# A fused two-layer decoder on one core: wide adds of GpSimd put on VectorE, the smaller expert scaled by the ratio of the weights, an output bias folded into a weight

## The reference

```
x = LN(x + scan_layer(x))          # in-projection, conv of 4 taps, selective scan over 16 states x 512 channels, out-projection
x = LN(x + cosine_scores(x, ctx))  # a 256x256 matrix of normalized dot products
x = LN(x + experts(x))             # softmax over 4 experts, the best 2 kept
x = LN(x + rotary_attention(x))    # 16 query heads, 4 key heads, width 64, low-rank terms
x = LN(x + cross_attention(x, ctx))
x = LN(x + gated_recurrence(x))    # c = f*c + i*g over the 8 batches; h = tanh(x wo' + c_final uo' + bo)
```

```
# experts: w is the softmax probability of the two best experts, 0 elsewhere
h   = relu(x Wi' + (x A_e') B_e')            # per expert e, width 1024
out = sum_e w_e * (h_e Wo')
# rotary: x1, x2 are the even and odd elements of a head
x1*cos - x2*sin , x1*sin + x2*cos
# cross attention: softmax(q k') v Wo + bo
```

## Time and profile before

| what | us |
| --- | --- |
| median of 3 runs | 1455.17 |
| lowest and highest | 1453.09, 1457.04 |
| the profiled execution's own time | 1455.81 |
| its span, first to last instruction | 1454.0 |
| PE busy / DVE busy / ACT busy / POOL busy in the span | 1267.8 / 1085.2 / 750.3 / 278.8 |
| mean granted TensorE clock | 0.945 of full |

### The profile page before, as it was taken

One profiled execution on the slowest core, in us unless ns is written; L12 is line 12 of the kernel. 1 busy time (PEld: TensorE's weight loads), 2 busy tenths in 40 slices (PEclk: granted clock), 3 DMA queues, 4 the chain that ended last, 5 costly groups with the idle time before them and its releaser, 6 DMA issues.

```text
span 1454.0 us, 17342 instructions
## 1 busy us (share of the span) xinstructions
PE 1267.8 (87%) x6336; PEld 1023.8 (70%) x6336; DVE 1085.2 (75%) x1750; ACT 750.3 (52%) x1637; POOL 278.8 (19%) x239
## 2 busy tenths in 40 slices
PE   3687788899999999999999999999998999899852
PEld 2454556677778787878787777878786878678732
DVE  2799699789977887788959988788778794333216
ACT  1543356365556655664647555665566454534421
POOL 0000124113301242112301231124211330130011
PEclk8877799999999999999999999999999999999967
DMA  4620110201020001100030102010010000000301
GB/s 162 218 76 19 48 38 30 65 1 58 1 99 1 30 30 35 65 30 29 8 92 1 59 0 99 1 30 30 27 66 30 30 8 26 1 0 8 114 0 58
DMA packets 27780, 62.63 MB, mean 43 GB/s; under 512 B 2360, under 2 KB 13720, under 8 KB 27056
## 3 DMA queue, kind: packets, MB, share of 16 engines
q1 hardware_dynamic: 27696, 61.53, 12.6%
HBM read 55.48 MB, written 6.04 MB: 42 GB/s over the span
## 4 chain that ended last, share of the span: by engine, by line
PE 46%; DVE 35%; issue 7%; ACT 7%; POOL 4%; DMA 1%; DVEq 0%; SPq 0%; ACTq 0%; POOLq 0%
PE bank L281 12%; DVE scans L491 10%; PE bank L442 7%; DVE scans L487 6%; PE bank L1066 4%; DVE scans L494 4%; PE bank L1111 4%; PE bank L624 3%; PE bank L1084 3%; PE bank L848 3%; DVE conv L381 2%; DVE nmax L1203 2%; PE bank L842 2%; PE bank L1073 2%; PE bank L579 1%
## 5 line engine op out<-in xcount | busy, mean ns | idle before, releaser
L491 DVE TENSOR_TENSOR_SCAN scans<-scans 128x1024 f32<-128x1024 f32 x128 | 303.2, 2368 | 7.2 <-ACT scans L465 4.9
L465 ACT ACTIVATE scans<-dt,a_neg 128x255 f32<-128x255 f32 x512 | 221.8, 502 | 111.6 <-DVE scans L491 111.4
L442 PE MATMUL bank<-scans,ident 128*128 128x256 f32 x1024 | 261.9, 402 | 19.3 <-DVE scans L494 19.2
L442 PEld LDWEIGHTS bank<-scans,ident 128*128 128x128 f32 x1024 | 198.1, 201 | 56.1 <-DVE scans L494 29.4
L487 DVE TENSOR_TENSOR scans<-conv,BC 128x1024 f32<-128x1024 f32 x128 | 168.3, 1315 | 24.6 <-PE bank L442 20.7
L1147 ACT ACTIVATE ya<-bank,nmax 128x256 f32<-128x256 f32 x256 | 107.0, 469 | 135.2 <-DVE nmax L1203 134.3
L494 DVE TENSOR_TENSOR scans<-scans,BC 128x1024 f32<-128x1024 f32 x128 | 168.9, 1319 | 2.1
L1203 DVE TENSOR_REDUCE nmax<-bank 128x2 f32<-128x512 f32 x128 | 87.4, 683 | 88.4 <-PE bank L1066 88.3
L1084 PE MATMUL bank<-v,ya 128*128 128x65 f32 x1024 | 129.1, 270 | 0.0
L1084 PEld LDWEIGHTS bank<-v,ya 128*128 128x128 f32 x1024 | 125.8, 193 | 1.7 <-issue 0.9
L778 POOL TENSOR_TENSOR wa<-wa 128x512 f32<-128x512 f32 x32 | 61.8, 1940 | 241.0 <-ACT wa L676 240.9
(11 more groups left out here) (255 smaller groups left out, 2192.0 us busy)
## 6 DMA issues: line engine op xcount, KB each, us to landing
BC<-xpj_scratch SPq DMA_DIRECT2D x32, 1024.0 KB, 5.4
xin<-in_x SPq DMA_DIRECT2D x8, 256.0 KB, 2.8
conv<-in_x SPq DMA_DIRECT2D x8, 256.0 KB, 2.8
out<-scans SPq DMA_DIRECT2D x8, 256.0 KB, 2.6
kept_x<-x SPq DMA_DIRECT2D x7, 256.0 KB, 2.0
kept_w<-wa SPq DMA_DIRECT2D x7, 256.0 KB, 2.1
BC<-kept_w SPq DMA_DIRECT2D x1, 1792.0 KB, 9.2
scans<-kept_x SPq DMA_DIRECT2D x1, 1792.0 KB, 13.4
```

The costliest lines, as they stand in the source:

```text
L442: last = pe.matmul(sums_of(c), ident[:, :], hb[u % 2][:, i, :], start=False, stop=(h == UH - 1 and i == HN - 1), skip_group_check=True)
L465: ins = act.activation(dA[u % 2][:, j, 1:S], dt[b % 2][:, c, 1:S], ACT.Exp, scale=a_neg[:, c, n:n + 1])
L491: dve.tensor_tensor_scan(flat(H[:, :, :]), flat(dA[u % 2][:, :, :]), flat(H[:, :, :]), 0.0, ALU.mult, ALU.add).then_inc(s["a_scan"], 1)
```

## The change

The experts' sum moves to VectorE. The second expert, whose weight is the smaller, is now made first: ScalarE writes relu of it times the ratio of the second weight to the first (with the largest logit subtracted, the best expert's exponential is 1, so the second largest exponential is that ratio). The best expert comes second, unscaled, and VectorE makes `max(z, 0) + hid` from the bank in one instruction. The best weight is applied at the residual, which becomes two instructions, one for each tile of tokens. ScalarE's second relu and GpSimd's add are gone, and the scores are no longer divided by their sum.

The rotary sums move to VectorE too. The two instructions of the sine half become one with a reversed middle axis, and the table `rope` is wider.

The output bias of the cross attention is added once, at the start, to row 64 of the second half of `w_vo`, which meets a feature that is always 1; the rows of the softmax sum to 1. GpSimd's add of the bias and its wait are gone.

All five strings of `ORDER` are new.

```diff
-                    act.activation(hid[:, j % 2, :], WB[j % 2][:, :], ACT.Relu, scale=sc2[:, 3, t:t + 1]).then_inc(s["f_r1"], 1)
-                    act.activation(r2[:, j % 2, :], WB[j % 2][:, :], ACT.Relu, scale=sc2[:, 5, t:t + 1]).then_inc(s["f_r2"], 1)
+                act.activation(hid[:, j % 2, :], WB[j % 2][:, :], ACT.Relu, scale=sc2[:, 5, j // 2:j // 2 + 1]).then_inc(s["f_r1"], 1)
...
-            own.link(dve.tensor_reduce(sc2[:, 1, :], sm[:, 1, :, :], AX, ALU.add))
-            own.link(dve.reciprocal(sc2[:, 2, :], sc2[:, 1, :]))
-            own.link(dve.tensor_tensor(sm[:, 2, :, :], sm[:, 1, :, :], wide(2), ALU.mult))
+            own.did(dve.tensor_reduce(sc2[:, 1, :], sm[:, 1, :, :], AX, ALU.add))
...
+            for j in range(4):
+                dve.wait_ge(*of("f_z2_ps", b, j + 1))
+                dve.scalar_tensor_tensor(hid[:, j % 2, :], WB[j % 2][:, :], 0.0, hid[:, j % 2, :], ALU.max, ALU.add).then_inc(s["f_h"], 1)
+                yield
...
-            dve.tensor_tensor(flat(x3[b % 2][:, :, :]), w0[:, :], flat(xb[:, :, :]), ALU.add).then_inc(s["f_res"], 1)
+            for t in range(T):
+                last = dve.scalar_tensor_tensor(x3[b % 2][:, t, :], w0[:, t * D:(t + 1) * D], sc2[:, 2, t:t + 1], xb[:, t, :], ALU.mult, ALU.add)
...
-                pool.tensor_tensor(hid[:, j % 2, :], hid[:, j % 2, :], r2[:, j % 2, :], ALU.add).then_inc(s["f_h"], 1)
...
-            pool.tensor_tensor(x4b[:, :, :], x3[b % 2][:, :, :], b_o1[:, :].unsqueeze(1).to_broadcast([P, T, D]), ALU.add).then_inc(s["c_x4b"], 1)
...
-                    pe.wait_ge(*of("t_rot", b, 6 + 3 * (n - 1)))
+                    pe.wait_ge(*of("t_rot", b, 4 + 2 * (n - 1)))
...
-                dve.tensor_tensor(out_sin[:, :, 0, :], x[:, :, 1, :], neg.to_broadcast(per), ALU.mult).then_inc(s["t_rot"], 1)
-                dve.tensor_tensor(out_sin[:, :, 1, :], x[:, :, 0, :], sin.to_broadcast(per), ALU.mult).then_inc(s["t_rot"], 1)
+                turned = x.rearrange("p h (b r) -> p h b r", b=2)[:, :, ::-1, :]
+                dve.tensor_tensor(out_sin.rearrange("p h (b r) -> p h b r", b=2), turned, sin.rearrange("p h (b r) -> p h b r", b=2),
+                                  ALU.mult).then_inc(s["t_rot"], 1)
...
+                    dve.tensor_tensor(keys[:, :, 0:S], cos_k, sin_k, ALU.add).then_inc(s["t_kr"], 1)
+                    dve.tensor_tensor(keys[:, :, S:S + HD], cos_k[:, :, 0:HD], sin_k[:, :, 0:HD], ALU.add).then_inc(s["t_kr"], 1)
...
+                    dve.tensor_tensor(queries[n % 2], rot[n % 2][:, 0, :], rot[n % 2][:, 1, :], ALU.add).then_inc(s["t_ro"], 1)
...
+            own.link(dve.tensor_copy(flat(w_vo[:, :, :]), w1[:, :]))
+            of_ones = w_vo[CTX - P:CTX - P + 1, 1, :]
+            dve.tensor_tensor(of_ones, of_ones, b_o1, ALU.add).then_inc(s["prep_evac"], 1)
...
     "pool": (
-        "FFFSWWWWWWFWYYYYYSWWWWWWWWYWWYYYYWYFSWWWWWWWWYWWYYYYYWFSWWWWWWWWYWWYYYYWYSFWWWWWWWWYWWYYYYWYFSWWWWWWWWYWWYYYYY"
-        "WSWWWWWWWWYWWYYYYYWSWWWWWWWWYWWYYYYYWWYWWWWW"
+        "FFFSWWWFSWWYFWWWWSWWYWWWFWSWWWWYWWFSWWWWYWWFSWWYWWWWSWWWWYWWSWWWWYWWWYWWWW"
```

More of the change, by code:

```diff
@@ L213, in build @@
         lowT = sb("lowT", [P, 2, S], F32R)
-        x4b, vo, qk, pe_c, pT_c, x1n = [wa[:, 2 * i:2 * i + 2, :] for i in range(6)]
+        vo, qk, pe_c, pT_c, x1n = [wa[:, 2 * i:2 * i + 2, :] for i in range(1, 6)]
+        b_o1 = wa[CTX - P:CTX - P + 1, 8, :]
         tg = wa[:, 0:6, :].rearrange("p (g k) s -> p g k s", g=3)
@@ L682, in kept_hidden @@
                                ACT.Copy).then_inc(s["f_hT"], 1)
-            weighed(0, 0)
+            second_expert(0)
             yield
-            weighed(1, 0)
+            second_expert(1)
             yield
-            for j in range(4):
-                weighed(j, 1)
+            for j in range(1, 4):
+                kept_hidden(j - 1)
                 yield
-                if j >= 1:
-                    kept_hidden(j - 1)
+                if j < 3:
+                    second_expert(j + 1)
                     yield
-                    if j < 3:
-                        weighed(j + 1, 0)
-                        yield
             kept_hidden(3)
@@ L735, in x_dve @@
             dve.wait_ge(*of("f_exp", b))
-            own.link(dve.tensor_reduce(sc2[:, 1, :], sm[:, 1, :, :], AX, ALU.add))
-            own.link(dve.reciprocal(sc2[:, 2, :], sc2[:, 1, :]))
-            own.link(dve.tensor_tensor(sm[:, 2, :, :], sm[:, 1, :, :], wide(2), ALU.mult))
-            for i, (score, hit, rank, one) in enumerate([(2, 3, 4, 5), (6, 7, 8, 9)]):
+            own.did(dve.tensor_reduce(sc2[:, 1, :], sm[:, 1, :, :], AX, ALU.add))
+            for i, (score, hit, rank, one) in enumerate([(1, 3, 4, 5), (6, 7, 8, 9)]):
                 top, best = 3 + 2 * i, 4 + 2 * i
@@ L746, in x_dve @@
                 if i == 0:
-                    own.link(dve.scalar_tensor_tensor(sm[:, 6, :, :], sm[:, 5, :, :], -2.0, sm[:, 2, :, :], ALU.mult, ALU.add))
+                    own.link(dve.scalar_tensor_tensor(sm[:, 6, :, :], sm[:, 5, :, :], -2.0, sm[:, 1, :, :], ALU.mult, ALU.add))
+                    own.did(dve.reciprocal(sc2[:, 2, :], sc2[:, 1, :]))
                 yield
-            own.link(dve.tensor_tensor(sm[:, 10, :, :], sm[:, 9, :, :], sm[:, 5, :, :], ALU.subtract))
+            own.link(dve.tensor_tensor(sm[:, 10, :, :], sm[:, 5, :, :], sm[:, 9, :, :], ALU.subtract))
             for t in range(T):
-                for i, one in enumerate([5, 10]):
+                for i, one in enumerate([9, 10]):
                     own.did(dve.tensor_tensor(low[:, i, t, :].rearrange("p (e r) -> p e r", e=NE),
@@ L762, in x_dve @@
                 dve.wait_ge(*of("l_kept_x", b - 2))
-            dve.tensor_tensor(flat(x3[b % 2][:, :, :]), w0[:, :], flat(xb[:, :, :]), ALU.add).then_inc(s["f_res"], 1)
+            for t in range(T):
+                last = dve.scalar_tensor_tensor(x3[b % 2][:, t, :], w0[:, t * D:(t + 1) * D], sc2[:, 2, t:t + 1], xb[:, t, :], ALU.mult, ALU.add)
+                if t == T - 1:
+                    last.then_inc(s["f_res"], 1)
+                else:
+                    own.did(last)
+            own.wait()
             dve.wait_ge(*of("f_res", b))
@@ L774, in x_pool @@
             yield
-            for j in range(4):
-                pool.wait_ge(*of("f_r1", b, j + 1))
-                pool.wait_ge(*of("f_r2", b, j + 1))
-                pool.tensor_tensor(hid[:, j % 2, :], hid[:, j % 2, :], r2[:, j % 2, :], ALU.add).then_inc(s["f_h"], 1)
-                yield
             pool.wait_ge(*of("x_var", b, 2))
```

126 lines of the change are left out of this document (54 added, 72 removed).

## The result

| | before | changed |
| --- | --- | --- |
| median, us (9 runs each) | 1454.59 | 1450.63 |
| lowest and highest | 1452.48, 1459.87 | 1449.38, 1451.40 |
| span of the profiled execution | 1454.0 | 1448.7 |

The ratio is 0.9968, with an interval of 0.9955 to 0.9980. The change brings 4.0 us by the medians, 4.7 by the ratio, 5.3 by the two spans, where 10.2 was forecast. The sign and the range hold the result; the size does not fit. What follows shows that this is the difference of two larger numbers: the edits alone are worth 14.4 us (13.8 by the ratio), and the new order takes some 10 of them away (9.7 by the medians, 9.2 by the ratios, with some 3 us either way).

A forecast was written before the change was run, and what follows sets the result against it. VectorE was taken to bound the kernel up to 275 us, TensorE after. VectorE's work +5.8, GpSimd's wait -12, ScalarE -3.0, experts' choice -1 make -10.2 on 1455.8: forecast 1445 us, 8-in-10 range 1427 to 1467.

The forecast's parts named there:

- VectorE's prices: Sums and products moved to VectorE: 0.69 us per 512-wide sum, reversed product at the straight price, 46.2 us added in all.
- Lengthening: Scan, L494 and L487 on VectorE: GpSimd's wide adds stretch them by 34.6 us, all given back; VectorE's net +11.6 us.
- rival A: GpSimd's small instructions keep part of the lengthening, only 15.3 of 34.6 us come back: 1455 us, chance 0.22.
- half of VectorE's time: VectorE has 35% of the chain and is 75% busy, so half of net +11.6 us sets the end: +5.8 us.
- GpSimd's wait, -12: TensorE's idle time ended by GpSimd's wide adds, 17.8 us: two thirds should go, -12 us, bounds 0 and -17.8.
- The sum without the order: Whole kernel: +5.8 - 12 - 3.0 - 1 = -10.2 us, with the new order costed at nothing.
- ScalarE and the choice: 32 relus gone from ScalarE, -3.0 us; two small dependent instructions gone ahead of the experts' low-rank product, -1 us.
- The order at nothing: New order strings of all engines: claimed to say the same where they count, 0 us, with 10 us to either side.
- The sign I had set for it: TensorE's start-up stretch ending later than 275 us by more than VectorE's added work there would show the order's doing.
- Rival B: Experts' sums wait for TensorE at the head of VectorE's list, some 0.69 us each: slower, 1472 us, chance 0.20.
- Rival C: All 17.8 us of waits go and scans on the path regain the whole 34.6: 1423 us, chance 0.08.

The follow-up runs named there:

- the idle adds: All edits in the old order, plus GpSimd wide multiplications nobody waits for at its adds' former places: 1470.11 us, against 1440.98 without them.
- all six kernels of the table: Before, changed, three steps put back, old start with new rest, new start with old rest, all old: 89.2 to 90.1 us for this stretch.

## Why the prediction was half right

**VectorE's prices: right.** The sums were put at 0.69 and measure 0.692 and 0.678; the reversed product was taken at the straight price and measures 0.680 against 0.681. VectorE's busy time was to be near 1097 and is 1087.8, 9 us less. Counted over all its kinds, each instruction that GpSimd ran beside less the median of those it did not, the lengthening before was 37.8 us rather than the 34.6 of the three kinds. The other 6 us of the difference were not followed.

**Lengthening: the mechanism right, its share of the path probably too small.** All of it went, as forecast, and rival A's shared lengthening does not exist: the small instructions on GpSimd stretch nothing. But half of VectorE's time was taken as on the path for both signs. For the added sums that nearly holds, 0.39 to 0.45 of 37.7 us. For the stretching by the idle adds it does not: 31.9 us cost 27.6, a share of 0.87. I read this as a matter of place, without a run of its own: the idle adds run where the experts and the rotary part go on, and the instruction they stretch there is one that TensorE's L442 waits for or that the next step of these parts stands behind. The 9.5 us in the sums of the keys are a case of it. In the kernel before, these sums were on GpSimd and 35.6 of the 37.8 us lay in the scan's three kinds, so 0.87 is not measured for its lengthening.

**GpSimd's wait, -12: its sum with the lengthening right, its own size not shown.** Taking the adds away brings 29.5 us where lengthening and wait were to make 29.3. That the sum fits says nothing on its terms. If the lengthening before cost 0.87 of itself, as the idle adds' does, it cost more than 29.5 alone and the waits were worth about nothing; the fit would be luck. If it cost the 0.45 of plain work, 17 us, the waits were worth the 12 of the forecast. No run separates the two. The two engines holding each other is also in the waits: the experts' add took 1.94 us on average, from 1.27 to 3.15, because it was held. The bias add L982, of the same size, always took 1.27 us; VectorE ran beside six of its eight, but only the products L1170, L1172 and L1173, which read one input from PSUM.

**The sum without the order: 10.2 forecast, 14.4 measured.** With the measured pieces it closes better: -29.5 for the adds, 0.39 to 0.45 of 46.2 (+18.0 to +20.8) for the work that VectorE gets, -3.0 and -1 as forecast for ScalarE and the choice: -15.5 to -12.7. The last two were not tried by themselves. The edits brought 4.2 us more than forecast; of that the added work accounts for 2.3 to 5.1, since 18.0 to 20.8 us stand where half of 46.2, 23.1, was put.

**The order at nothing: wrong, and this is the step that failed.** "The order strings are new, but where they count they say the same. ... I cost the new order at nothing, with 10 us to either side." The comparison was made by the place of three things among VectorE's scans: two residuals, of batch 0 and of batch 6, and the last scan. None of them looks at what TensorE does ahead of the first scan, nor at the steps between the scans of batch 1, and a shift of one scan (26 for 25) was taken as none. The places that decide are the first 60 us and batch 1's scan, in the regime that the prediction's own first paragraph called VectorE's. A late `w_xp` moves everything behind it: from the first L487 to the end of batch 0's scan all six kernels of the table need 89.2 to 90.1 us, so nothing is caught up. The new strings cost 9.7 us (1450.63 against 1440.98), at the very edge of the bound given.

**The sign I had set for it was blind.** The prediction said that the order would show if the start-up stretch ended later than 275 us. It ended at 275.9, against 274.8 before, which looks like nothing. But the edits shorten that stretch by themselves: with the edits and the old order it ends at 266.3. The loss was hidden by a gain at the same place, and only the windows gave it away, with 106.2 us of VectorE's work done by 145 us instead of 108.9.

**Rival B, experts' sums waiting at the head of VectorE's list: did not happen.** 5.4 us over 32 of them, 0.17 each, where it needed 0.7. In the run with the old order it is 9.4 us, 0.29 each, and that run is the faster one. **Rival C** thought that the scans on the path would get their lengthening back whole and all 17.8 us of waits go besides. The two together would be 52.4 us, where the wide adds are worth 29.5 in all.

## What to carry to other kernels

Where an engine's instruction is stretched by a neighbour, count the stretched time at its place and not by the engine's average share of the path: here 0.87 of it set the end with idle adds put beside the work, and some 0.4 of plain added work. Where a change brings new fixed orders with it, follow the first transfer that the bounding engine waits for step by step through both orders; two letters at the start were worth 4 to 5 us, about as much as the whole change had brought. Time a change in the old order as well as in its own: here that version, 1440.98 us, beats both kernels.
